# Turning normalised tiles as 32x32 squares (VectorE and two DMAs) in the feed-forward stages of a conditioned transformer block

## What is computed

```python
# layer 0
norm = _layernorm(x) * (1.0 + scale[:, None]) + shift[:, None]
norm = jnp.where(m, norm, 0.0)
ssm_out = jnp.where(m, gelu(norm@ssm_w1)@ssm_w2 + gelu(norm@bwd_w1)@bwd_w2, 0.0)
x = x + gate_msa[:, None] * ssm_out
ff_norm = _layernorm(x) * (1.0 + scale_mlp[:, None]) + shift_mlp[:, None]
x = x + gate_mlp[:, None] * (gelu_tanh(ff_norm @ ff_w1 + ff_b1) @ ff_w2 + ff_b2)
# layer 1
x = x + attention(modulate(layernorm(x))) @ wo      # 16 heads of 32
xn = _modulate(_layernorm(x, ln2_w, ln2_b), shift_f, scale_f)
x = x + gelu(xn @ w1 + b1) @ w2 + b2                # w1: 512 x 2048
```

## Time and profile before

| | |
|---|---|
| time, median of 3 runs | 2103.26 us (2102.76 to 2105.36) |
| the profiled execution's own time | 2103.58 us |
| its span, first to last instruction | 2101.8 us |
| TensorE matmul busy | 2051.0 us (98%) |
| VectorE busy | 1197.6 us (57%) |
| ScalarE busy | 661.9 us (31%) |
| GpSimd busy | 366.7 us (17%) |
| granted TensorE clock, mean | 0.998 of 2.4 GHz |
| DMA traffic | 160.92 MB, mean 77 GB/s |

### The profile page before, as it was taken

How to read it: one execution, slowest core, us unless ns; L and a number is a source line. 1 busy time by engine, 2 the same in 40 slices (tenths; PEclk the granted TensorE clock), 3 DMA queues, 4 the chain that set the end, 5 groups by cost and what they waited for, 6 DMA issues and landing times. The chain is left out here.

```text
span 2101.8 us, 32450 instructions
## 1 busy us (share of the span) xinstructions
PE 2051.0 (98%) x11066; PEld 1698.2 (81%) x11066; DVE 1197.6 (57%) x2212; ACT 661.9 (31%) x2006; POOL 366.7 (17%) x427
## 2 busy tenths in 40 slices
PE   6999999999999998999999999989999999999999
PEld 4787778888888878888888888778888888888887
DVE  5566666655555557888888888862423324233322
ACT  3222222222222223555555555541212112121211
POOL 4232332222222211111111111110100101010200
PEclk9999999999999999999999999999999999999999
DMA  7532222233222223232323233240010101101000
GB/s 256 194 105 95 95 95 90 100 118 131 95 94 95 90 86 99 75 90 72 92 70 88 77 83 82 81 131 13 29 41 1 40 0 40 38 2 40 0 21 20
DMA packets 99718, 160.92 MB, mean 77 GB/s; under 512 B 9964, under 2 KB 43336, under 8 KB 97608
## 3 DMA queue, kind: packets, MB, share of 16 engines
q1 hardware_dynamic: 90248, 130.17, 19.8%
q0 software_dynamic: 9360, 29.96, 4.6%
q10 hardware_dynamic: 48, 0.00, 0.0%
HBM read 109.23 MB, written 34.08 MB: 68 GB/s over the span
## 5 line engine op out<-in xcount | busy, mean ns | idle before, releaser
L553 PE MATMUL mlp_m<-xn,weights 128*128 128x512 f32 x1536 | 378.3, 397 | 5.6 <-DVE xn L783 5.6
L576 PE MATMUL ffn_y<-weights,ffn_h 128*128 128x512 f32 x1536 | 377.3, 395 | 1.6 <-DVE ffn_h L796 1.6
L576 PE MATMUL mlp_y<-weights,mlp_h 128*128 128x512 f32 x1536 | 376.4, 395 | 1.2 <-DVE mlp_h L796 1.2
L553 PE MATMUL ffn_m<-xn,weights 128*128 128x512 f32 x1536 | 372.2, 392 | 2.8 <-PEq L145 2.8
L576 PEld LDWEIGHTS ffn_y<-weights,ffn_h 128*128 128x128 f32 x1536 | 288.3, 188 | 70.6 <-DVE ffn_h L796 2.0
L576 PEld LDWEIGHTS mlp_y<-weights,mlp_h 128*128 128x128 f32 x1536 | 288.2, 188 | 70.6 <-issue 2.1
L553 PEld LDWEIGHTS mlp_m<-xn,weights 128*128 128x128 f32 x1536 | 286.1, 190 | 65.4 <-DVE xn L783 6.0
L553 PEld LDWEIGHTS ffn_m<-xn,weights 128*128 128x128 f32 x1536 | 286.2, 188 | 63.2 <-issue 3.2
L794 DVE CAST ffn_h<-ffn_g 128x512 fp32r<-128x512 f32 x128 | 56.5, 441 | 382.2 <-ACT ffn_g L692 382.2
L692 ACT ACTIVATE ffn_g<-ffn_m,vecs 128x512 f32<-128x512 f32 x128 | 88.1, 688 | 500.3 <-PE ffn_m L553 494.8
L1160 PE MATMUL att_banks<-xn,weights 128*128 128x256 f32 x1536 | 197.5, 287 | 10.8 <-PEq L145 5.8
(11 more groups left out here) (135 smaller groups left out, 2103.0 us busy)
## 6 DMA issues: line engine op xcount, KB each, us to landing
x_tiles<-x SPq DMA_DIRECT2D x132, 256.0 KB, 2.8
x<-x_tiles SPq DMA_DIRECT2D x96, 256.0 KB, 2.1
mlp_bias<-gate_bias_rows POOLq DMA_DIRECT2D x64, 256.0 KB, 3.5
mlp_gate<-gate_rows SPq DMA_DIRECT2D x16, 1024.0 KB, 5.0
att_kdiag<-xn SPq DMA_DIRECT2D x128, 128.0 KB, 2.5
x_tiles<-in_x_dram SPq DMA_DIRECT2D x32, 256.0 KB, 5.0
out_dram<-x_tiles SPq DMA_DIRECT2D x32, 256.0 KB, 2.1
mlp_stage<-in_L_cond_ff_w_dram POOLq DMA_DIRECT2D x16, 256.0 KB, 4.0
```

The source lines that it names most:

```text
L553: last = nc.tensor.matmul(m1_ps[:, c % 2, :], st.tiles[0](a, k, c), xn[:, parity, b, k, :], start=s == 0, stop=s == len(steps) - 1)
L576: last = nc.tensor.matmul(y_ps[:, tile, :], h[:, c % 2, a, tile * P:(tile + 1) * P], st.tiles[1](b, c), start=c == 0 and s == 0, stop=c == ...
```

## The change

In all blocks but the first of the `mlp` phase (whose four tiles keep the old way, as `first_turn`), the turn of a tile no longer goes through TensorE and PSUM:

- `normalise` writes `xhat` with its columns permuted, so that each group of 32 columns holds features 4 apart. Behind it on VectorE a transpose of the 32x32 squares in place (one instruction on 128x512).
- SyncE, in a new `swap_squares`: waits for that transpose, stores the tile in DRAM, waits until the store has landed, waits until the tile before has been split out of `xmod`, and loads it back with the blocks exchanged: 128 partitions with 4 runs of 128 numbers (512 bytes) each.
- `modulate` waits for the load and works in place in `xmod`, in SBUF, four instructions with 4 runs of 32 numbers. It moves one step later (c = t+3), and so does `split_xn` (c = t+4), which now reads runs of 32.
- The next `normalise` waits for the store, where it had waited for TensorE's turn.

```diff
+            def swap_squares(n, tile):
+                sp.wait_ge(squares_turned, swaps(n, tile) + 1)
+                sp.sem_inc(passed, 1)
+                sp.dma_start(sh.squares_dram[tile], xhat[:, :]).then_inc(squares_stored, 16)
+                sp.wait_ge(squares_stored, 16 * (swaps(n, tile) + 1))
+                sp.sem_inc(passed, 1)
+                if not reached(ln(TPB * n + tile)):
+                    sp.wait_ge(xn_ready, ln(TPB * n + tile))
+                    sp.sem_inc(passed, 1)
+                sp.dma_start(xmod_sq[:, :, :, :].rearrange("p a k t -> p a (k t)"),
+                             sh.squares_dram[tile].rearrange("(a i) (q m) -> (i q) a m", a=NSQ, q=NSQ)).then_inc(squares_loaded, 16)
...
                         sp.wait_ge(gates_stored, 128)
                         load_gate(stages[0], 0)
+                        for tile in range(TPB):
+                            swap_squares(1, tile)
...
                 load_next(2)
                 load_next(3)
+                if after is not None:
+                    for tile in range(after.token_tiles):
+                        swap_squares(n + 1, tile)
...
-                    if after is not None and TURN_STEP <= c < TURN_STEP + after.token_tiles:
-                        turn(n + 1, c - TURN_STEP)
...
-                    if after is not None and TURN_STEP <= c < TURN_STEP + after.token_tiles:
-                        modulate(after, n + 1, c - TURN_STEP)
+                    if after is not None and TURN_STEP + 1 <= c <= TURN_STEP + after.token_tiles:
+                        modulate(after, n + 1, c - TURN_STEP - 1)
...
+                    if not in_opening(n - 1) or tile:
+                        dve.wait_ge(squares_stored, 16 * swaps(n, tile))
...
+                    source = source.rearrange("p (k i q) -> p q k i", k=KC, q=NSQ)
+                    target = target.rearrange("p (q k i) -> p q k i", q=NSQ, k=KC)
+                nc.vector.tensor_scalar(target, source, mv[:, tile, 0:1], r, ALU.subtract, ALU.mult).then_inc(xhat_ready, 1)
+                if not in_opening(n):
+                    dve.wait_ge(xhat_ready, ln(row + 1))
+                    nc.vector.transpose(xhat[:, :], xhat[:, :]).then_inc(squares_turned, 1)
...
-                        if TURN_STEP + 1 <= c <= TURN_STEP + after.token_tiles:
-                            split_xn(n + 1, 1 - parity, c - TURN_STEP - 1)
+                        if TURN_STEP + 2 <= c < TURN_STEP + 2 + after.token_tiles:
+                            split_xn(n + 1, 1 - parity, c - TURN_STEP - 2)
```

More of the change, by code:

```diff
@@ L238, in mlp_phase @@
     reached = lambda count: isinstance(count, int) and count < 1
+    swaps = lambda n, tile: TPB * (n - 1) + tile
+    in_opening = lambda n: isinstance(n, int) and n == 0
     following = stages[-1].following
@@ L522, in _, with first_turn @@
         def _(pe):
[L523 to L530, removed]
+            def first_turn(tile):
+                pe.wait_ge(xhat_ready, tile + 1)
+                if tile >= 2:
+                    pe.wait_ge(modulated, tile - 1)
                 for k in range(KC):
-                    last = nc.tensor.transpose(turn_ps[:, tile % 2, k * P:(k + 1) * P], source[:, k * P:(k + 1) * P], sh.ident[:, :])
+                    last = nc.tensor.transpose(turn_ps[:, tile % 2, k * P:(k + 1) * P], xhats[tile % 2][:, k * P:(k + 1) * P], sh.ident[:, :])
                 last.then_inc(turned, 1)
@@ L634, in first @@
                     for tile in range(TPB):
-                        turn(0, tile)
+                        first_turn(tile)
             def block_step(n, parity, before, st, after):
@@ L670, in modulate @@
                 row = batch_row(st, n, tile)
-                act.wait_ge(turned, ln(TPB * n + tile + 1))
+                if in_opening(n):
+                    act.wait_ge(turned, tile + 1)
+                else:
+                    act.wait_ge(squares_loaded, 16 * (swaps(n, tile) + 1))
                 if room and st.order == 1 and isinstance(n, int) and row == 0:
@@ L675, in modulate @@
                     act.wait_ge(sh.table_loaded[following.phase], 16)
[L676 to L682, removed]
-                for k in range(KC):
-                    last = nc.scalar.activation(target[:, k, :], turn_ps[:, tile % 2, k * P:(k + 1) * P], ACT.Identity,
+                if in_opening(n) and tile >= 2:
+                    act.wait_ge(xn_ready, tile - 1)
+                for k in range(KC):
+                    if in_opening(n):
+                        target, source = xmods[tile % 2][:, k, :], turn_ps[:, tile % 2, k * P:(k + 1) * P]
+                    else:
+                        target = source = xmod_sq[:, :, k, :]
+                    last = nc.scalar.activation(target, source, ACT.Identity,
                                                 bias=sh.tables[:, st.table, 1, k, bass.ds(row, 1)], scale=sh.tables[:, st.table, 0, k, bass.ds(row, 1)])
@@ L765, in normalise @@
                     r = rstd_m[:, tile:tile + 1]
-                target = xhat
-                if isinstance(n, int) and n == 0:
-                    target = xhats[tile % 2]
+                source, target = x[:, parity, tile, :], xhat[:, :]
+                if in_opening(n):
+                    target = xhats[tile % 2][:, :]
                     if tile >= 2:
                         dve.wait_ge(turned, tile - 1)
-                elif not reached(ln(row)):
-                    dve.wait_ge(turned, ln(row))
@@ L781, in split_xn @@
-                nc.vector.tensor_copy(hi, source[:, :, :]).then_inc(xhi_done, 1)
+                hi, lo = (xn[:, parity, part, :, tile * P:(tile + 1) * P] for part in (HI, LO))
+                source = xmods[tile % 2]
+                if not in_opening(n):
+                    hi, lo = (half.rearrange("p k (a t) -> p k a t", a=NSQ) for half in (hi, lo))
+                    source = xmod_sq[:, :, :, :].rearrange("p a k t -> p k a t")
+                nc.vector.tensor_copy(hi, source).then_inc(xhi_done, 1)
@@ L782, in split_xn @@
                 dve.wait_ge(xhi_done, ln(TPB * n + tile + 1))
[L783 to L784 removed]
+                nc.vector.tensor_tensor(lo, source, f32(hi), ALU.subtract).then_inc(xn_ready, 1)
             def split_h(n, c):
```

26 lines of the change are left out of this document (13 added, 13 removed).

## The result

The changed kernel takes **2106.86 us** (median of 20 runs, 2104.43 to 2109.52), the kernel before 2102.23 (20 runs, 2100.11 to 2105.36). The ratio is 1.0022, with a 95% interval of 1.0015 to 1.0029: slower by 0.22%. Forecast was 2096, faster by 0.35%.

What follows compares the result with a forecast made beforehand. TensorE, busy 98% of the span, was taken as the bound. Turns saved -38.5, block-end stalls +15.4, `mlp` block 0 +15 and `ffn` block 0 +0.7 sum to -7.4 us: 2096 us, range 2079 to 2124.

Steps and rivals of the forecast that it cites:

- handover loop: Per tile through `xmod`: SyncE's reaction, load, modulate, split_xn; 6.2 us against TensorE's step of 5.52.
- Block 0, +15: First `mlp` block: the store of squares waits behind the gate load, delaying normalise(1) and second(4); +15 us, once.
- the rival in which block 0 doesn't hold the store: `mlp` block 0: gate transfer and store mix, 9.8 us less, 2086 us in all; chance 0.08.
- The stall: Block ends in `mlp`: split_h(0) ready at T7+11.7, wanted by second(0) at T7+10.85; 0.9 us per block.
- "add 0.4": Masked blocks 1 to 7: a VectorE instruction lengthened beside GpSimd's, expected at split_h(6); 1.3 us stall per block.
- a sign of a loop over 6.4: TensorE's waits for `xn` longer than those for `mlp_h` would show the forecast wrong.
- slow handover rival: Block ends: a loop over 6.4 us, stalls of 1.6 per block eat all; at 6.8, 2121 us; chance 0.29.
- "Nothing else moves much": Argument against a slower loop: little else moves on the queues in steps 5 to 7.
- A turn at 0.47: Each turned tile costs TensorE 0.47 us; 82 of them removed give -38.5 us.
- Block 0 of `ffn`, +0.7: First `ffn` block, VectorE nearly full: 2.6 us of stall, less 4 turns saved; +0.7 us.
- VectorE as the bound: Rival: about 63 us more on VectorE, busy 57%, matters only at block ends and `ffn` block 0; no chance given.
- the quick handover: Rival: load 3.0 us or less, loop 5.85 or shorter, block-end stalls nearly vanish; 2082 us; chance 0.28.

Runs made afterwards that it cites:

- e3: Changed kernel with block 0's last two weight loads and gate load issued on ScalarE's queue instead of SyncE's: 2106.37 us, ratio 1.0024 to before.
- e4: Changed kernel with a second room for the returning squares in the `mlp` phase, so a load waits for the tile before the last: 2078.68 us.
- e7: Kernel before with the 90 turns of the later blocks left out on TensorE (output differs), the ceiling for freeing TensorE of them: 2057.91 us.
- e9: Changed kernel loading the squares in one 2 KB run per partition instead of 4 of 512 bytes (output differs): 2100.84 us, ratio 0.9996 to before.
- b2: Changed kernel with both repairs: block 0's tiles turned by TensorE, and two rooms for the squares in `mlp`: 2061.62 us, ratio 0.9804 to before.
- e8: Changed kernel with 32 semaphore increments nobody waits for on TensorE ahead of its `ffn` work: 2108.03 us, ratio 1.0036 to before.
- e1: Changed kernel with squares in the `ffn` phase alone, the `mlp` phase being that of the kernel before: 2090.13 us, ratio 0.9947 to before.
- e10: Changed kernel with GpSimd's last addition in attention held until VectorE's last weight piece there is done: 2106.26 us, ratio 1.0026 to before.
- e5: Changed kernel with the four tiles that `mlp` block 0 prepares turned by TensorE, as before: 2089.31 us, ratio 0.9933 to before.

## Why the prediction was wrong

The step that failed is the handover loop in the masked stage. The forecast took the second stage's loop of 6.2 us and added 0.4 per block for one collision; the loop there is 6.9, and blocks 1 to 8 gave back 1.3 us instead of 5.0. Alone this doesn't turn the sign. Three terms that were put at nothing, or at a gain that didn't come, do it together: attention, the pauses in `ffn`, and block 15. One by one:

- **Block 0, +15: right in size, half right in cause.** It was 14.8, the wait of VectorE in front of normalise(1) 16.4. second(4) came at 73.4, not 76, but a second wait (2.46) and two groups at a low clock (4.74 and 4.59 instead of 2.96) made up for it, so the exact hit is partly luck. That the order in the queue is the cause fell with e3: the rival in which block 0 doesn't hold the store was to give 9.8 back, and with the store landed 7.3 us earlier 1.1 came back, since the load behind it then took 8.6.
- **The loop of 6.2 us: right as a sum.** In the second stage the median distance from load to load is 6.2. The parts erred in opposite directions: in the medians the load is 2.8 in place of 3.35, SyncE's reaction 0.1 in place of 0.25 and the modulation 1.65 in place of 1.35, with 0.2 between landing and modulation; that makes 5.9, and the rest are single loads of 3 to 4.5 us. The stall was forecast at 0.9 per block and is 0.9 (45.11 against 44.21).
- **The masked stage, "add 0.4": the step that failed.** The collision of the earlier trace rows was taken as one at split_h(6), behind the loop. What GpSimd does lengthens the loop itself: in blocks 4 and 5 its addition lies over split_xn, in the others its bias transfer mostly goes ahead of the load. The median distance from load to load is 6.9, so split_xn(3) comes late for first(0) itself (15.7 us of waits for `xn`, 5.6 of them the opening's), which the forecast gave as a sign of a loop over 6.4. The miss is 3.7 us over blocks 1 to 8. That is the slow handover rival, in 7 blocks of 14, and with a reason it named: the load beside a bias transfer of GpSimd's. "Nothing else moves much" was what spoke against it, and it was wrong in the masked stage.
- **A turn at 0.47: right.** It is 0.46 in the `mlp` phase and in `ffn`. But the two turns of block 15 brought nothing (51.0 us from its start to attention's, 51.1 before), 0.9 us.
- **Block 0 of `ffn`, +0.7: too dear.** It is 0.5 shorter than before (91.8 against 92.3), with waits of 1.48 and 0.96 us for `ffn_h` against 1.61.
- **Put at nothing:** 2.9 us of pauses in `ffn`, which some neighbours of the kernel don't have, and 2.4 us in attention, which the change doesn't touch; and the 3.1 us by which the medians lie further apart than the profiled executions. The forecast had no term for the place of the code or for a clock that falls elsewhere.
- **VectorE as the bound: rightly small.** In e4 it is busy 89 us more than before, and the second stage's blocks take 44.21, as in e7 without any turn.
- **The 512-byte rule** of the Trainium skill ("DMA: Bandwidth & Descriptors", Specifications), by which 512 bytes are enough for line rate, was set aside for the window at 188 GB/s. e9 puts the truth nearer the rule: 0.2 us in landing, not 0.55. But the quick handover that it led to (2082) did not follow, since the modulation took back most of what the load gave, and single loads took 3 to 4.5 us.
- **The rule on 128x128 transposes** of the Trainium skill ("VectorE: DVE Perf Modes", Rules for kernel authors), which gives them to TensorE, doesn't hold for this kernel as a whole: in b2, 32x32 squares and two transfers, in all but the first two blocks of the `mlp` phase, are 2.0% faster.

The sign turned because a gain of 38.5 and losses of 31 were to leave -7.4, and errors of 3.7 (the masked stage), 3.3 (block 15 and attention) and 1.9 us (`ffn`) all lay on one side. With a sum of so many terms that nearly cancel, a sign is worth little.

## What to carry to other kernels

When a value's way back is lengthened, count the rooms it can wait in before counting the instructions: here a second place for the tile, 2 KB per partition, was worth 28 us, nearly as much as the change was to gain by the turns (38.5). A loop that is tighter than the engine it feeds passes on everything that lengthens one of its parts, here about 1.0 us by an instruction on another engine or by another transfer; both belong into the sum once per turn of the loop. Keep small transfers that something waits for out of a stretch in which megabytes move; another queue does not shelter them, a different way of doing the step does.

## What the hardware showed that was not expected

- Instructions in `ffn` were fetched again, or not, by where TensorE's code lay: 51 packets on the instruction queue against 33 or 34, and 2.9 us (2.0 of them idle), turned off by 32 idle instructions (e8), and by nothing in the `ffn` code itself (e1 against the changed kernel).
- A 256 KB load of squares lands after 2.74 us in the median, and after 3.71 where another engine's 256 KB transfer was issued in the 2 us before it; beside 3 MB on another queue it took 8.6 (e3).
- An activation in place in SBUF, reading and writing 4 runs of 32 numbers, takes 483 ns, from PSUM to SBUF 456. A normalise that reads every fourth number takes 738 instead of 545 ns in `ffn`.
- Behind a pause of TensorE of the same length, 1.56 us at the end of attention, the next 12 matmuls took 3.0 us in before, e1 and e10 and 4.6 in b2 and e5. In the seven kernels with a pause of 1.98 to 2.47 us there they took 4.3 to 5.5.
